# A small GpSimd memset behind every gather of a graph network kernel, and two range-checked loads

## The reference, cut to what matters

```python
# three layers of this, with leaky_relu slope 0.01
deg = segment_sum(ones, col); norm = deg**-0.5[row] * deg**-0.5[col] * edge_weight
xw  = einsum('ni,tio->tno', x, W)            # one table of rows for each of four types
out = segment_sum(xw[edge_type, col] * norm[:, None], row) + b
x1  = layernorm(x + (x + z1 + z2 + z3) / 4)
# one attention layer, two heads of 64
xp    = (x1 @ W).reshape(n, 2, 64)
alpha = leaky_relu(a_src[src] + a_dst[dst], 0.2)
e     = exp(alpha - segment_max(alpha, dst)[dst])
out   = segment_sum(e / s[dst] * xp[src], dst) + bias
result = layernorm(x1 + out)
```

## Time and profile before

| what | value |
|---|---|
| median of 3 runs | 8958.33 us (8957.9 to 8960.3) |
| the profiled execution, first to last instruction | 11925.3 us; the profile gives no other time for it |
| POOL busy, of that span | 6395.8 us (54%) |
| PE, DVE, ACT busy | 5307.0, 4574.2, 3992.0 us |
| mean granted TensorE clock | 0.634 of full speed |
| first gather of the layers starts at | 691.47 us |
| first gather of the attention starts at | 8505.49 us |

### The profile page before, as it was taken

The page is one execution under the profiler, slowest core; times in us unless marked ns, Lnnn a source line. Parts: engine busy times, 40 slices in busy tenths (PEclk is TensorE's granted clock), DMA queues, the critical chain, the costliest instruction groups (busy, mean ns, idle before and its releaser), DMA issues.

```text
span 11925.3 us, 149378 instructions
## 1 busy us (share of the span) xinstructions
PE 5307.0 (45%) x32765; PEld 4105.0 (34%) x32766; DVE 4574.2 (38%) x12940; ACT 3992.0 (33%) x12236; POOL 6395.8 (54%) x6521
## 2 busy tenths in 40 slices
PE   5843434434533434343433434343444444444444
PEld 4632322223322323232322323232344444444444
DVE  9952222222322212222322222222555555555556
ACT  6522222222322222222322222222455454445455
POOL 1656566565456565656466565656344444444443
PEclk9975655656655655565655556555566666666666
DMA  1011111111221111111211111111122222222222
GB/s 47 35 42 43 41 44 43 41 44 41 65 55 44 40 44 40 44 40 44 76 42 44 40 44 40 44 40 44 49 69 70 68 71 69 69 68 69 70 69 65
DMA packets 432687, 612.42 MB, mean 51 GB/s; under 512 B 232038, under 2 KB 249491, under 8 KB 432539
## 3 DMA queue, kind: packets, MB, share of 16 engines
q0 software_dynamic: 208832, 428.96, 13.7%
q1 hardware_dynamic: 223707, 182.02, 4.6%
HBM read 437.29 MB, written 51.28 MB: 41 GB/s over the span
## 4 chain that ended last, share of the span: by engine, by line
another core or an unknown queue 48%; DVE 16%; issue 15%; PE 8%; ACTq 5%; DVEq 4%; ACT 3%; POOL 0%; DMA 0%; POOLq 0%; SPq 0%
DVEq L1604 3%; PE bank L1196 3%; ACT g_step L912 3%; ACTq L896 2%; DVE a_miss L1717 2%; PE wide L1196 2%; DVE g_hot L1620 2%; ACTq L912 1%; DVE acc L1634 1%; DVE a_max L1722 1%; DVE lo_hot L1262 1%; DVE acc L1788 1%; PE bank L1191 1%; DVE v_hot L1387 1%
## 5 line engine op out<-in xcount | busy, mean ns | idle before, releaser
L737 POOL DMA_INDIRECT g_rows<-gcn_table,rec_idx x4743 | 4487.1, 946 | 2894.2 <-ACT g_step L912 1484.6
L912 ACT ACTIVATE g_step<-g_rows,rec_w 128x128 f32 x5580 | 1791.5, 390 | 5679.7 <-remote 4618.4
L762 POOL DMA_INDIRECT a_roll<-gat_table,src_plane x1612 | 1524.6, 946 | 1801.0 <-ACT a_cand L937 1375.4
L1634 DVE TENSOR_TENSOR acc<-acc,bank 128x512 f32 x930 | 637.9, 686 | 3828.8 <-remote 3238.9
L1191 PE MATMUL bank<-zeros 1*128 1x512 bf16 x930 | 490.9, 528 | 2909.9 <-DVE acc L1634 2104.6
L1196 PE MATMUL bank<-g_step,g_hot 128*128 128x128 f32 x7440 | 1621.7, 386 | 128.4 <-issue 50.6
L1196 PEld LDWEIGHTS bank<-g_step,g_hot 128*128 128x128 f32 x7440 | 1391.8, 280 | 487.9 <-issue 487.9
L1222 PE MATMUL bank<-a_msg,a_hot 128*128 128x130 f32 x3608 | 798.9, 389 | 1648.7 <-DVE a_msg L1768 1635.0
L1222 PEld LDWEIGHTS bank<-a_msg,a_hot 128*128 128x128 f32 x3608 | 685.6, 283 | 1786.3 <-DVE a_msg L1768 1452.3
L1191 PEld LDWEIGHTS bank<-zeros 1*128 1x128 bf16 x930 | 89.9, 97 | 3099.0 <-DVE acc L1634 2163.3
L937 ACT ACTIVATE a_cand<-a_miss,a_rows 128x128 f32<-128x128 bf16 x3608 | 1095.9, 386 | 14.9 <-DMA a_rows<-a_roll 8.8
(11 more groups left out here) (272 smaller groups left out, 5880.3 us busy)
## 6 DMA issues: line engine op xcount, KB each, us to landing
a_rows<-a_roll SPq DMA_DIRECT2D x451, 264.0 KB
g_rows<-gcn_table,rec_idx POOLq DMA_INDIRECT x4743
gcn_table<-rows SPq DMA_DIRECT2D x147, 256.0 KB
a_roll<-gat_table,src_plane POOLq DMA_INDIRECT x1612
e_dst<-by_dst_dst SPq DMA_DIRECT2D x451, 2.0 KB
gat_table<-acc SPq DMA_DIRECT2D x7, 462.0 KB
out_x<-xs SPq DMA_DIRECT2D x6, 448.0 KB
gcn_slots<-nothing SPq DMA_DIRECT2D x4, 468.0 KB, 6.8
```

The costliest lines, as they stand in the source:

```text
L737: pool.indirect_dma_start(out=g_rows[:, tile % RING, :], out_offset=None, in_=gcn_tables[layer % 2], in_offset=bass.IndirectOffsetOnAxis(a ...
L762: pool.indirect_dma_start(out=a_roll[:, g % ROLL, t, :], out_offset=None, in_=gat_table, in_offset=bass.IndirectOffsetOnAxis(ap=src_plane[ ...
L912: last = nc.scalar.activation(g_step[:, j, k, :].unsqueeze(1), g_rows[:, bass.ds(slots[k], 1), :], ACT.Copy, scale=rec_w[:, bass.ds(q.at(0 ...
L1634: V.tensor_tensor(dst_ap, dst_ap, sums_of(j).rearrange("p (k d) -> p k d", k=GP), ALU.add).then_inc(s_gadd, 1)
```

## The change

Behind each of the 6448 gathers GpSimd writes a memset of 128 x 1 fp32 into a new tile `pace`. It increments a new semaphore `s_pause`; from the second on each memset first waits for the one before it. Besides, the number `tile` that ScalarE's wait on `s_land` uses is loaded with a load and a range check of its own, apart from the four slots; SyncE loads `tile` and `slot` with two loads, each with a range check, where it was one load without.

```diff
+        pace = sb("pace", [P, 1])
+        s_pause = sem("s_pause")
...
-                    _, (tile, slot) = nc.values_load_multi_w_load_instructions(
-                        gat_at[0:1, bass.ds(q.at(0), 1), :].rearrange("p g k -> p (g k)"),
-                        engines=(mybir.EngineType.SP,), min_val=0, max_val=GAT_GROUPS - 1,
-                        skip_runtime_bounds_check_because="a step less the begun blocks, at most the last group")
-                    slot = nc.s_assert_within(slot, 0, ROLL - 1,
-                                              skip_runtime_bounds_check_because="a group modulo the ring")
+                    tile = sp.value_load(gat_at[0:1, bass.ds(q.at(0), 1), 0], min_val=0, max_val=GAT_GROUPS - 1)
+                    slot = sp.value_load(gat_at[0:1, bass.ds(q.at(0), 1), 1], min_val=0, max_val=ROLL - 1)
...
+            paused = [0]
+
+            def pause():
+
+                if paused[0]:
+                    pool.wait_ge(s_pause, paused[0])
+                nc.gpsimd.memset(pace[:, :], 0.0).then_inc(s_pause, 1)
+                paused[0] += 1
...
                             ).then_inc(s_g[t // 4], 16)
+                            pause()
                             n = q * len(FOURS) + t // 4
...
                     ).then_inc(s_g[g % ROLL], 16)
+                    pause()
...
                 def slots_of(q):
+                    tile = act.value_load(gcn_at[32:33, bass.ds(q.at(0), 1), GP], min_val=0,
+                                          max_val=CH * CCOLS - 1)
                     _, values = nc.values_load_multi_w_load_instructions(
-                        gcn_at[32:33, bass.ds(q.at(0), 1), :].rearrange("p g k -> p (g k)"),
-                        engines=(mybir.EngineType.Activation,), min_val=0, max_val=CH * CCOLS - 1,
-                        skip_runtime_bounds_check_because="a step less the begun blocks, at most the last tile")
-                    return values
+                        gcn_at[32:33, bass.ds(q.at(0), 1), 0:GP].rearrange("p g k -> p (g k)"),
+                        engines=(mybir.EngineType.Activation,), min_val=0, max_val=RING - 1,
+                        skip_runtime_bounds_check_because="a tile modulo the ring")
+                    return *values, tile
```

More of the change, by code:

```diff
@@ L895, in slots_of @@
                 def slots_of(q):
+                    tile = act.value_load(gcn_at[32:33, bass.ds(q.at(0), 1), GP], min_val=0,
+                                          max_val=CH * CCOLS - 1)
                     _, values = nc.values_load_multi_w_load_instructions(
-                        gcn_at[32:33, bass.ds(q.at(0), 1), :].rearrange("p g k -> p (g k)"),
-                        engines=(mybir.EngineType.Activation,), min_val=0, max_val=CH * CCOLS - 1,
-                        skip_runtime_bounds_check_because="a step less the begun blocks, at most the last tile")
-                    return values
+                        gcn_at[32:33, bass.ds(q.at(0), 1), 0:GP].rearrange("p g k -> p (g k)"),
+                        engines=(mybir.EngineType.Activation,), min_val=0, max_val=RING - 1,
+                        skip_runtime_bounds_check_because="a tile modulo the ring")
+                    return *values, tile
                 def scale(q, values):
                     j = q.slot(0) % 3
[L904 to L907, removed]
+                    *slots, tile = values
                     if q.live(-3) or layer:
```

## The result

| what | value |
|---|---|
| changed kernel, median of 4 runs | 9056.73 us (9054.48 to 9057.78) |
| kernel before, same chip, 4 runs | 8958.15 us (8957.9 to 8960.3) |
| ratio, 95% interval | 1.0109 (1.0095 to 1.0124) |
| profiled execution, first to last instruction | 9054.4 us |

The change costs 98.6 us, 1.1%. I had forecast 484 us: the sign was right, the size five times too large. And the profiled execution takes as long as the others, although the profile holds 164027 instructions where that of before held 149378. So recording costs nothing here, and the 2967 us by which the profile of before was longer must come from elsewhere.

What follows compares the result with a forecast made beforehand. The prediction took GpSimd's 6448 gathers, 1.25 us apart, as the bound. It added 484 us for memsets and nothing for waits and checked loads to 8958.33 us: 9442 us, 5.4% slower, range 8950 to 9850.

Steps and rivals of the forecast that it cites:

- The sum 11925.3 - 1484.6 - 1375.4: Profiled span of the kernel before less GpSimd's two waits for ScalarE: 9065.3 us, 1.2% over the median of 8958.33.
- the price of recording so many instructions: Inferred cause of ScalarE's slow register work and late steps in the profile, 2967 us longer than the median.
- I take the middle, 0.075 us: Cost of each memset between two gathers on GpSimd, midway between 0.03 and 0.12 us: 484 us over 6448.
- the plain case: Each memset adds between its spacing, 0.03 us, and its whole duration, 0.12 us, to GpSimd: 193 to 774 us.
- the rival of the free memset: Memsets fit into the 0.30 us between gathers on GpSimd and cost nothing: 8958 us; chance 15%.
- the full hand-over: Each change between gather and memset on GpSimd costs 0.30 us again: from 9732 up to 11537 us; chance 10%.
- the shorter gap: A memset replaces a penalty between adjacent gathers on GpSimd: 7217 us at full price, 8088 at half; chance 8%.
- ScalarE or VectorE: Rival: these engines set the attention's pace and cover its memsets: 9321 us; no separate chance, inside the likeliest range.
- I take the waits at nothing: Each memset's wait for the previous memset on GpSimd costs nothing, as the sequencer keeps about one gather, 1.25 us, of lead.
- the upper bound of the memsets: Whole duration of 0.12 us per memset if the next gather on GpSimd doesn't overlap with it: 774 us.
- the case without cover: Checked loads not hidden behind GpSimd's work: ScalarE's 1395 would cost 432 us; with cover taken at nothing.
- the likeliest case: Memset on GpSimd's path at 0.03 to 0.12 us each: 9442 us, own range 9151 to 9732; chance 67%.

Runs made afterwards that it cites:

- runs 9 to 12: Changed kernel with, in turn: each memset waiting for the fourth before it, 8943.14 us; eight memsets per gather, 10043.44; waiting for the second before, 8952.41; for itself, 10774.91.
- run 9: Changed kernel with the memsets in four columns, each waiting for the fourth before it: 8943.14 us, beside 8943.44 for the kernel before.
- run 12: Changed kernel with the wait behind each memset and for that same memset, so no lead: 10774.91 us, beside 8942.68 for the kernel before.
- run 1: Changed kernel without its memsets and their waits, only the checked loads left: 12185.3 us, beside 11931.47 for the kernel before.
- run 10: Changed kernel with eight memsets behind every gather instead of one, lead still one gather: 10043.44 us, beside 8943.44 for the kernel before.

## Why the prediction was right or wrong

**What bounds the kernel: right, with a wrong reason beside it.** That GpSimd's spacing of 1.25 us sets the pace is borne out: each of runs 9 to 12 moves by what its gathers are apart, and no other engine's time. The sum 11925.3 - 1484.6 - 1375.4 that I took as the test of it came out near the median; but the cause I named, "the price of recording so many instructions", is refuted. The profiled executions take as long as the others on either kind of chip, and the kernel before takes 11931 us on the hampered ones. The waits for ScalarE were, by all that the runs show, real time on a hampered chip. That the sum told what the kernel is bound by was luck in part: it rested on the wrong cause.

**The memsets: wrong.** The step "I take the middle, 0.075 us" should read 0. The bounds came from memsets behind memsets and left out of the plain case what the rival of the free memset said: the engine idles 0.30 us between gathers, and 0.12 us fit in. Against it I held that the gap stays the same with the sequencer far ahead, so that it looks like the gather's own work. The gap is the same 0.30 us with the memset inside, so if it is the gather's own work, a memset can be done meanwhile. That rival had 15% and its term was the right one: 484 us forecast, nothing measured (run 9). The Trainium skill's rules, timing by the spacing of starts (Perfetto Trace Analysis, section GPSIMD Engine Instruction) and completion that doesn't hold back the next instruction (GPSIMD Engine Reference, section Instruction dispatch), pointed the nearer way, 9151 against 9732. Even the spacing, though, is paid only from the memset that no longer fits. The rivals of the full hand-over and of the shorter gap fell with the spacing of 1.25 us, and ScalarE or VectorE doesn't set the pace in the attention: of the 355.0 us before the gathers of L770, 351.2 are waits for nobody.

**The waits: wrong, and this is the whole result.** "I take the waits at nothing" is 97 to 99 us. I asked what must fit into a lead of 1.25 us, looked at the instructions that the trace shows there (0.017 us, and 0.31 us in the attention, where with the register work it is 0.455) and found that they fit. The step that failed is to take these durations for the time that the sequencer needs: with no lead the gathers behind them are held up by 0.64 and 1.20 us (run 12). The 1.20 do not always fit into a lead of one: some 18 us. And once in some 88 gathers something holds the next gather up by over a gather's time without any instruction to show for it.

The trace of before could have shown this. Most of the 73 gathers keep their 1.25 us there, under the lead of the earlier trace rows, but 21 of them, 18 of these in the attention, come 0.6 to 1.4 us late. There GpSimd has waited for ScalarE at one of the last five gathers, and so its sequencer has lost lead:

```profile
9430.66 0.94 POOL L762 DMA_INDIRECT a_roll<-gat_table,src_plane  x1 [10.93 <-ACT a_cand L937]
9433.29 0.94 POOL L762 DMA_INDIRECT a_roll<-gat_table,src_plane  x1 [1.69 <-issue]
```

The sum had no term for a lead cut from over two gathers to one. The text gave a price for each wait without cover, about 0.30 us, and let the upper bound of the memsets stand for it. Run 12, which has no cover, bears that price out on average (1832.2 / 6448 = 0.28 us), but as a mean of 0.08 us for most gathers and far more for those behind a hand-on or a load.

**The checked loads: right where GpSimd sets the pace** (run 9 contains them at no cost), and wrong on a hampered chip, where ScalarE is on the path: 254 us (run 1), of the order of the 432 us that I gave for the case without cover.

**The range** of 8950 to 9850 held the time, but by luck. It reached so far down only for the rival of the free memset; the likeliest case's own range, 9151 to 9732, missed it. And the sum has two errors of opposite sign: a cost too many of 484 us and one too few of 98.

What stays open: what it is that comes once in some 88 gathers, at the same gathers in every one of these kernels (it is neither the loading of instructions nor something that comes by time, as run 10 shows), and what sets the two kinds of chips apart.

## What to carry to other kernels

Price a wait on an engine's own last result by the lead that it takes from the sequencer: here four gathers of lead cost nothing, two 10 us, one 98 us and none 1832 us over 6448 gathers. If a chain of waits on GpSimd must stay, let each wait look two to four links back, with a column of the tile for each. Price what a sequencer does from a stretch in which it has no lead, not from the durations of its instructions. And where a profiled span is far longer than the times beside it, run the kernel before once more before drawing on that trace: the two may come from chips, or states of a chip, that differ.

## What the runs showed of the hardware that I had not expected

- One 128x1 memset between two indirect gathers of 128 rows costs nothing that can be measured: 1.25 us from gather to gather with and without it, 1.30 with four memsets, 1.41 with eight.
- The same 73 of the 6448 gathers come late in every kernel with a lead of one, 85 to 89 gathers apart, although nothing in the trace holds GpSimd: by 0.64 to 1.49 us in the changed kernel, by at most 0.54 with a lead of two, and by nothing with four. Seven more memsets behind each gather don't move them to other gathers (run 10).
- The sequencer's rows understate what its work holds up: 0.64 us behind a pass of 0.017, 1.20 behind a load, its register work (together 0.455) and two passes (run 12).
- Two chips on which the kernel before takes 11931 to 11936 us instead of 8943 to 8958. There some register instructions of ScalarE's sequencer take up to 1.4 us instead of 0.074, and kernels that gather more slowly are faster: 11333 us at 1.30 us between gathers, 10920 at 1.33 and more. Recording a profile costs nothing on either kind (9054.4 us of span beside a median of 9056.73; 12175.4 beside 12185.3).
